# Layer 1's query-key matrices built during layer 0's fill, with the waits at the kernel's start rearranged

## The reference, cut to what matters

```python
# layer 1, attention (H = 16 heads, D = 128)
y = jnp.einsum('bnd,hde->bhne', x, Wkqv) + bkqv[None, :, None, :]
k, q, v = y[..., :D], y[..., D:2 * D], y[..., 2 * D:]
A = jnp.einsum('bhnd,bhmd->bhnm', q, k) / jnp.sqrt(jnp.float32(D))
A = softmax(where(causal, A, -inf))
out = einsum('bhnm,bhmd->bnhd', A, v).reshape(B, N, D) @ Wp + bp
```

## Time and profile before

| | us |
|---|---|
| median of three runs | 2234.11 |
| lowest, highest | 2232.35, 2235.26 |
| profiled execution | 2234.54 |
| its span, first to last instruction | 2232.8 |

### The profile page before, as it was taken

How to read it: one execution, slowest core, us unless ns; L and a number is a source line. 1 busy time by engine, 2 the same in 40 slices (tenths; PEclk the granted TensorE clock), 3 DMA queues, 4 the chain that set the end, 5 groups by cost and what they waited for, 6 DMA issues and landing times. The chain is left out here.

```text
span 2232.8 us, 60806 instructions
## 1 busy us (share of the span) xinstructions
PE 2053.9 (92%) x16256; PEld 1529.6 (69%) x16256; DVE 1781.3 (80%) x5918; ACT 1557.9 (70%) x3951; POOL 1117.5 (50%) x2439
## 2 busy tenths in 40 slices
PE   5999999996899999999999999999999993999990
PEld 3666666664677766766776776676777672999990
DVE  6899999993488888888888888888888884777775
ACT  2565656564588777878877887887777872777774
POOL 5777777775123444444344344444434434444444
PEclk7999999999899999999999999999999996999995
DMA  1000000000100000000000000000200001222226
GB/s 35 25 21 28 21 28 21 28 23 21 43 2 2 11 11 4 9 11 9 4 12 11 2 11 11 6 7 11 86 3 12 11 2 37 61 66 65 64 61 226
DMA packets 63638, 62.91 MB, mean 28 GB/s; under 512 B 9834, under 2 KB 58613, under 8 KB 62855
## 3 DMA queue, kind: packets, MB, share of 16 engines
q1 hardware_dynamic: 54906, 42.64, 6.3%
q0 software_dynamic: 8448, 16.93, 2.3%
HBM read 33.17 MB, written 22.69 MB: 25 GB/s over the span
## 5 line engine op out<-in xcount | busy, mean ns | idle before, releaser
L1373 DVE SCALAR_TENSOR_TENSOR restT<-ps_t,leadT 128x512 f16<-128x512 f32 (+1 forms) x768 | 458.7, 597 | 136.0 <-ACT leadT L1300 106.1
L1300 ACT ACTIVATE leadT<-ps_t 128x512 f16<-128x512 f32 (+1 forms) x768 | 402.2, 524 | 138.0 <-PE ps_t L1166 137.0
L1149 PE MATMUL ps_s<-xT_all,qm 128*128 128x512 f32 (+1 forms) x1024 | 489.8, 560 | 0.8 <-ACT qm L1281 0.8
L1166 PEld LDWEIGHTS ps_t<-ident,p 128*128 128x128 f32 x2560 | 316.0, 141 | 233.2 <-issue 169.4
L1166 PE MATMUL ps_t<-ident,p 128*128 128x128 f32 x2560 | 413.4, 276 | 8.0 <-DVE restT L1373 6.3
L1291 ACT ACTIVATE p<-ps_s,neg_max 128x512 f32<-128x512 f32 (+1 forms) x512 | 325.6, 636 | 80.3 <-DVE neg_max L1363 67.4
L1363 DVE CUSTOM_DVE_ANT_0 ps_s<-ps_s,mask 128x512 f32<-128x512 f32 (+1 forms) x512 | 319.9, 625 | 44.4 <-PE ps_s L1149 43.1
L993 POOL CAST v_parts<-v_all 128x36 bf16<-128x36 f32 x256 | 56.9, 222 | 562.8 <-PE ps_o L1180 562.8
L1149 PEld LDWEIGHTS ps_low<-xT_all,qm 128*128 128x128 f32 x1024 | 194.8, 190 | 135.7 <-issue 122.4
L1140 PE MATMUL ps_qm<-xT_all,m_head 128*128 128x512 f32 x512 | 264.2, 598 | 0.3 <-issue 0.3
L262 POOL TENSOR_TENSOR pv_prod<-probs,kv 128x2048 f32<-128x2048 f32 x64 | 259.3, 4072 | 3.8 <-POOL probs L254 2.3
(11 more groups left out here) (222 smaller groups left out, 4198.2 us busy)
## 6 DMA issues: line engine op xcount, KB each, us to landing
row_in<-rows_dram SPq DMA_DIRECT2D x136, 65.0 KB
y<-results SPq DMA_DIRECT2D x16, 512.0 KB, 5.2
xT<-in_xT SPq DMA_DIRECT2D x32, 128.0 KB, 2.1
xres<-in_xT SPq DMA_DIRECT2D x32, 128.0 KB, 2.1
xT_all<-x2T SPq DMA_DIRECT2D x32, 128.0 KB, 2.0
out_x<-x SPq DMA_DIRECT2D x16, 256.0 KB, 3.4
xT_all<-in_wide SPq DMA_DIRECT2D x1, 2760.0 KB
results<-row_out,row_in POOLq DMA_INDIRECT x136
```

The source lines that it names most:

```text
L1149: mm = pe.matmul(ps_s[n], qm[j][:, n * P:(n + 1) * P], xT_all[:, bass.ds(b * S, (n + 1) * P)], start=True, stop=True)
L1166: mm = pe.transpose(ps_t[g][:, at + n * P:at + (n + 1) * P], probs[i][:, n * P:(n + 1) * P], ident[:, :])
L1300: act.activation(leadT[j][g][:, :], ps_t[g][:, 0:width[g]], ACT.Copy, scale=RAISE)\
L1373: dve.scalar_tensor_tensor(out=restT[j][g][:, :], in0=ps_t[g][:, 0:width[g]], scalar=RAISE, in1=leadT[j][g][:, :], op0=ALU.mult, op1=ALU.s ...
```

## The change

1. `wq`, `wk`, `bq` are loaded by SP in layer 0, after step 0's DMAs, on a semaphore `qk_weights_in`. PE builds the matrices and the bias column at the head of its step 1 (`build_matrices`), in the banks `ps_y`, `ps_tail` and `ps_front`, which the fill does not use yet; ACT copies them at the head of its step 1 (`copy_matrices`). `project` of pair 0 waits for the four copies, `four_experts` of pair 0 for the bias. `m_all` and `mb_all` live through the stages.
2. POOL makes the constants first and sets `v_all` after them; `copy_v` of pair 0 waits for it. `consts_made` counts five.
3. `wqkv` has a semaphore of its own. PE's first four products wait for it and `xT` alone; the constants and the seven other weights are waited for after them. ACT no longer waits for the constants.
4. In `attention1` PE reads each head's matrix from `m_all`; `m_head` and `load_head` are gone. POOL splits the first head's values before it makes the route's constants, and DVE squares the centroids after the masks of head 0.

```diff
@@ layer0, SP @@
+                    if first(u, j, 0):
+                        for dst, src in ((wq, wqT), (wk, wkT), (bq_sb, bq)):
+                            sp.dma_start(dst[:, :], src).then_inc(qk_weights_in, 16)
-                sp.dma_start(wqkv_sb[:, :], wqkv).then_inc(weights_in, 16)
+                sp.dma_start(wqkv_sb[:, :], wqkv).then_inc(wqkv_in, 16)
@@ layer0, POOL @@
-                pool.memset(v_all[:, :], 1.0).then_inc(consts_made, 1)
+                pool.memset(ident[:, :], 0.0).then_inc(ident_zeroed, 1)
...
-                pool.memset(ident[:, :], 0.0).then_inc(ident_zeroed, 1)
                 pool.wait_ge(ident_zeroed, 1)
...
-                pool.wait_ge(consts_made, 6)
+                pool.memset(v_all[:, :], 1.0).then_inc(v_set, 1)
+                pool.wait_ge(consts_made, 5)
@@ layer0, PE @@
-                pe.wait_ge(consts_made, 6)
-                pe.wait_ge(weights_in, 16 * NWEIGHTS)
+                pe.wait_ge(wqkv_in, 16)
+
+                def build_matrices():
+                    pe.wait_ge(qk_weights_in, 16 * 3)
+                    for g in range(H // 4):
+                        for h in range(4 * g, 4 * g + 4):
+                            mm = pe.matmul(tile(ps_m[g], h % 4), tile(wq, h), tile(wk, h), start=True, stop=True)
+                        mm.then_inc(m_ps, 1)
+                    pe.wait_ge(m_sb, 1)
+                    for h in range(H):
+                        mm = pe.matmul(ps_m[0][:, h:h + 1], tile(wk, h), bq_sb[:, h:h + 1], start=True, stop=True)
+                    mm.then_inc(mb_ps, 1)
...
+                    if first(u, j, 0):
+                        pe.wait_ge(m_sb, H // 4)
...
+                    if first(u, j, 1):
+                        build_matrices()
...
                 qkv_products(0, 0, 0)
                 qkv_products(0, 0, 1)
+                pe.wait_ge(consts_made, 5)
+                pe.wait_ge(weights_in, 16 * NWEIGHTS)
                 steps(pe, step)
@@ layer0, ACT @@
-                act.wait_ge(consts_made, 6)
...
+                def copy_matrices():
+                    for g in range(H // 4):
+                        act.wait_ge(m_ps, g + 1)
+                        act.copy(m_all[:, g * 4 * P:(g + 1) * 4 * P], ps_m[g][:, :]).then_inc(m_sb, 1)
+                    act.wait_ge(mb_ps, 1)
+                    act.mul(mb_all[:, :], ps_m[0][:, 0:H], SCALE).then_inc(mb_sb, 1)
+
                 def step(u, j, part):
+                    if first(u, j, 1):
+                        copy_matrices()
@@ attention1 @@
-                pool.wait_ge(m_sb, H // 4)
-
-                def load_head(b, h):
-                    k = H * b + h
-                    j = h % 2
-                    when(pool, qm_ps, k - 1)
-                    pool.sem_inc(passed, 1)
-                    pool.tensor_copy(m_head[j][:, :], m_all[:, h * P:(h + 1) * P])\
-                        .then_inc(m_head_ready, 1)
...
                 def queries(b, h):
                     k = H * b + h
                     j = h % 2
-                    pe.wait_ge(m_head_ready, k + 1)
                     when(pe, qm_sb, k)
-                    pe.matmul(ps_qm[:, :], m_head[j][:, :], xT_all[:, bass.ds(b * S, S)],
+                    pe.matmul(ps_qm[:, :], blk(m_all, h), xT_all[:, bass.ds(b * S, S)],
                               start=True, stop=True).then_inc(qm_ps, 1)
```

More of the change, by code:

```diff
@@ L63, in __init__, with layer0 @@
         assert self.chunk * self.chunks == hidden and self.blocks == 4
-def layer0(nc, sh, xT_in, wqkv, wproj, bproj, gate_w, gate_b, expert_w, expert_b, wv1, keep):
-    xT_all, v_all, ident, ones = keep
+def layer0(nc, sh, xT_in, wqkv, wproj, bproj, gate_w, gate_b, expert_w, expert_b, wv1, wqT, wkT, bq, keep):
+    xT_all, v_all, ident, ones, m_all, mb_all = keep
+    SCALE = float(P) ** -0.5
     NP = sh.tiles // 2
@@ L144, in layer0 @@
         ident_zeroed = sem("ident_zeroed")
-        weights_in = sem("weights_in")
+        weights_in, wqkv_in, v_set = sem("weights_in"), sem("wqkv_in"), sem("v_set")
+        qk_weights_in, m_ps, m_sb, mb_ps, mb_sb = (
+            sem("qk_weights_in"), sem("m_ps"), sem("m_sb"), sem("mb_ps"), sem("mb_sb"))
         xT_loaded = [sem(f"xT_loaded{j}") for j in range(2)]
@@ L188, in before, with first @@
             return u + (j - k) // 2, (j - k) % 2
+        def first(u, j, s):
+            return isinstance(u, int) and 2 * u + j == s
         v_heads = v_all[:, :].rearrange("p (b h k c) -> p b h k c", h=H, k=sh.blocks, c=DH + 1)
@@ L368, in four_experts @@
                     s = 2 * u + j
+                    if first(u, j, 0):
+                        pe.wait_ge(mb_sb, 1)
                     when(pe, gated_ready, 4 * s + 2 * a + half - 1)
@@ L546, in copy_v @@
                     act.wait_ge(v_ps, s + 1)
+                    if first(u, j, 0):
+                        act.wait_ge(v_set, 1)
                     for a in range(2):
@@ L588, in _ @@
             def _(dve):
-                dve.wait_ge(consts_made, 6)
+                dve.wait_ge(consts_made, 5)
                 def by_head(t, n=H):
@@ L753, with attention1 @@
 NOWHERE = 1 << 22
-def attention1(nc, sh, wqT, wkT, bq, wp, wpT, bp, bv1, cT, keep, routing, expert_loads):
-    xT_all, v_all, ident = keep
+def attention1(nc, sh, wp, wpT, bp, bv1, cT, keep, routing, expert_loads):
+    xT_all, v_all, ident, m_all, mb_all = keep
     rows_dram, tile_expert, tile_row = routing
@@ L781, in sem @@
             return ctx.enter_context(nc.semaphore(name))
-        wq = sb("wq_sb", [P, H * P])
-        wk = sb("wk_sb", [P, H * P])
-        bq_sb = sb("bq_sb", [P, H])
-        m_all = sb("m_all", [P, H * P])
-        mb_all = sb("mb_all", [P, H])
-        m_head = [sb(f"m_head{j}", [P, P]) for j in range(2)]
         mask = sb("mask", [P, S])
@@ L1120, in _ @@
             def _(pe):
-                pe.wait_ge(weights_in, 48)
-                for g in range(H // 4):
-                    for h in range(4 * g, 4 * g + 4):
-                        mm = pe.matmul(ps_m[g][:, (h % 4) * P:(h % 4 + 1) * P], wq[:, h * P:(h + 1) * P],
-                                       wk[:, h * P:(h + 1) * P], start=True, stop=True)
-                    mm.then_inc(m_ps, 1)
-                for h in range(H):
-                    mm = pe.matmul(ps_qm[:, h:h + 1], wk[:, h * P:(h + 1) * P], bq_sb[:, h:h + 1],
-                                   start=True, stop=True)
-                mm.then_inc(mb_ps, 1)
-                pe.wait_ge(m_sb, H // 4)
-                pe.wait_ge(mb_sb, 1)
                 def queries(b, h):
@@ L1267, in _ @@
             def _(act):
-                for g in range(H // 4):
-                    act.wait_ge(m_ps, g + 1)
-                    act.copy(m_all[:, g * 4 * P:(g + 1) * 4 * P], ps_m[g][:, :]).then_inc(m_sb, 1)
-                act.wait_ge(mb_ps, 1)
-                act.mul(mb_all[:, :], ps_qm[:, 0:H], SCALE).then_inc(mb_sb, 1)
-                act.wait_ge(mb_sb, 1)
                 def copy_queries(b, h):
@@ L1950, in two_layers @@
             v_all = three_stages.enter_context(nc.sbuf_tensor("v_all", [P, sh.tiles * H * (DH + 1)], F32))
-            layer0(nc, sh, xT, wqkv, wproj, bproj, gate_w, gate_b, expert_w, expert_b, wv1,
-                   (xT_all, v_all, ident, ones))
+            m_all = three_stages.enter_context(nc.sbuf_tensor("m_all", [P, H * P], F32))
+            mb_all = three_stages.enter_context(nc.sbuf_tensor("mb_all", [P, H], F32))
+            layer0(nc, sh, xT, wqkv, wproj, bproj, gate_w, gate_b, expert_w, expert_b, wv1, wqT, wkT, bq,
+                   (xT_all, v_all, ident, ones, m_all, mb_all))
             wide_sb = xT_all[:, 0:E * sh.wide]
@@ L1957, in two_layers @@
             expert_loads = ((wide_sb, wide), (w2_sb, w2))
-            attention1(nc, sh, wqT, wkT, bq, wp, wpT, bp, bv1, cT, (xT_all, v_all, ident), routing,
+            attention1(nc, sh, wp, wpT, bp, bv1, cT, (xT_all, v_all, ident, m_all, mb_all), routing,
                        expert_loads)
```

70 lines of the change are left out of this document (32 added, 38 removed).

## The result

The changed kernel takes 2211.49 us, the median of four runs (2207.62 to 2212.74); the kernel before, in four runs beside it, 2233.47 (2232.35 to 2235.26). The ratio is 0.9895, interval 0.9882 to 0.9908, so the change takes 22 us away. Forecast were 2210.5 us and a range of 2205 to 2218. The profiled execution took 2211.51 us with a span of 2209.8, 23.0 less than that of before.

What follows compares the result with a forecast made beforehand. It took PE to fill the loops, leaving the layer boundary and first 40 us, where no engine is full. Boundary -19.0, loop 0, start -6.2, build +1.5 gave -23.7: 2210.8, or 2210.4 against the median; stated 2210.5, range 2205 to 2218.

Steps and rivals of the forecast that it cites:

- The boundary: Between layer 0 and layer 1: first query product directly after the barrier, at 555.65 instead of 574.64, gaining 19.0 us.
- +-1.3: Layer 1's first products: PE's clock rising sooner wins 1.3 us, later loses 1.0; zero was taken.
- The start: Kernel's start: PE waits only for `wqkv` and `xT`, starting at about 3.6 instead of 9.83, gaining 6.2 us.
- DVE's term: Kernel's start: DVE's first product follows PE at the same distance, at 7.1 instead of 13.34.
- The step by which ACT's table load follows PE at the same distance as in before: Kernel's start: ACT's table load and copy keep their distance behind PE's first product, so DVE starts at 7.1.
- The bound of 2.9 us for DVE beside the clear of `v_all`: Kernel's start: DVE's first product overlaps POOL's clear from 7.1 to 10; the whole overlap bounds the loss.
- The build in the fill: Layer 0's fill: matrices built on PE from 13.5 to 24.2, making the head sums late by 1.5 us.
- the prediction's bounds, 0 and 6.8: Lateness in layer 0's fill: 0 with full clock from 24; 6.8 us with half clock through the build too.
- The loop: Layer 1's loop: removing 256 POOL copies gains 0; bounds 3 us won, 1 us lost.
- rival (b): Layer 1's loop: without POOL's copies 4 to 8 us of PE's stalls go, total 2204; chance 0.08.
- Rival (a): Layer 0's fill: the build eats the start's gain, lateness 6 us instead of 1.5, total 2215; chance 0.20.
- Rival (d): Layer 1's query products: reading from `m_all` exposes PE's weight load, costing 49 us, total 2259; chance 0.02.

Runs made afterwards that it cites:

- A: Chip of the result and of the profile before: kernel before 2233.47 us, changed kernel 2211.49 us.
- C: Chip of the second group of follow-up runs: kernel before 2234.20 us, changed kernel run again 2210.69 us, ratio 0.9891.
- D: Chip of the third group of follow-up runs: kernel before 2234.53 us; changed kernel with `m_head` put back 2209.30 us (one run).
- B: Chip of the first group of follow-up runs: kernel before 2257.18 us; changed kernel with `m_head` put back 2234.68 us, ratio 0.9900.

## Why the prediction was right

**The boundary: right to the tenth.** Forecast -19.0 with 1.3 either way for the clock; 18.97 measured. The first product follows the barrier at once, 2.2 us behind the end of ACT's last copy, and nothing that was moved (the constants, the centroids' squares, the five DMAs) made DVE late: its first mask came 5.1 us behind the first product, in before 5.2. The clock: after, half speed lasted until 559.2, 7.6 us behind the first product, where it was 8.2 in before; the loop is as long as before. So neither end of the +-1.3 was used.

**The start: PE right, DVE's term mis-sized by 1.3 us.** PE at 3.69 for 3.6. The step by which ACT's table load follows PE at the same distance as in before failed. In before the table load came behind PE's first product; in after it is at 0.79. The run with ACT's wait put back shows the cause: with that wait, DVE starts at 7.31. The Trainium skill, "ScalarE: Activation LUTs" (What ACT_TABLE_LOAD costs), measures 1283 ns for the load, and this trace's 1.28 us agrees; its step-by-step section says that the compiler puts the load right before the activation, and the traces add which wait stands in front of it. The start without the build was worth 7.3 us at the first statistics instead of 6.2.

The bound of 2.9 us for DVE beside the clear of `v_all` was not needed: DVE's two products took 4.49 us beside POOL's 7.77 us clear, as they did alone in before. By the Trainium skill, "SBUF — State Buffer" (Who interferes with whom), a DVE instruction with at most one SBUF input, outside its two-port modes, doesn't contend with GpSimd; the trace agrees, for a clear that only writes. The same page's rule on two SBUF inputs was weighed in the prediction by the division into `sa`, which ran 172 to 192 ns with the copies and 173 to 192 without. That row can't test the rule: in before none of the 256 divisions overlaps a copy of `m_head` (the copy at 1000.07 ends at 1000.36, the division next to it starts at 1001.29). What shows no price of the copies on A, by this rule or another, is the loop, 1266.4 us with the copies and 1266.5 without.
```profile
L1389 DVE TENSOR_TENSOR sa<-out_sum,recip x256: 173/181/192, 568.8 to 1829.7; 128x32 f32<-128x32 f32 x128
```

**The build in the fill: the mechanism right, the size wrong.** The prediction named the queue (build, qkv products, sums, qkv products, sums) and worked out two sizes: 3.4 us late with the clock at half throughout, and 1.5 if it rose in the first sums. It took 1.5. The build's own length held (14.79 to 25.5, 10.7 us, as put). Measured are 3.6 on A (34.28 against 30.67) and 4.7 on C. The term that was mis-sized is the clock's: the prediction expected a single rise, by the one in before at 33.3. What came was a rise in the build and a fall in the bias products. Also, `bq` landed at 14.79, 1.3 later than put. With the same order on PE the lateness was 0.3 and 0.6 us on D, where the clock stayed full, and 1.3 and 1.7 on B. So 1.5 lies within what this stream does, but no single value could have been right for it; the prediction's bounds, 0 and 6.8, hold all of them.

**The loop: right on A, for a reason that was only half seen.** Nobody waits for the copies, so 0: that held, with +0.1 us. But a wait list with no entry tells that the cover suffices, not how thick it is. It was 0.2 us a head here. On B POOL goes on 0.5 us later after each scatter, and there the kernels without the copies have a loop 13 to 14.5 us shorter than those with them: rival (b), more than it allowed for, on another chip. There the kernel with only ACT's wait restored was 37.5 us faster than before, where before and after differ by 22 on A.

**The sum.** -19.0 and 0 held; start and build, -6.2 + 1.5 = -4.7, came as -7.3 + 3.6 = -3.7, and -4.0 at the barrier. Two errors of over 1 us in opposite directions left 0.7 in the sum, 2211.5 for 2210.8 in the profiled execution. That the total was within 1 us is therefore better than its terms deserve. Rival (a), the build eating the start's gain, happened in part: 3.6 us of lateness where it had 6. Rival (d), an exposed weight load, did not: PE's loads for the query product take 192 ns in the median and 190 to 191 with the copies, and the loop is as long.

## What to carry to other kernels

A step that is in no wait list still has a margin: read how long before its use it ends (here 0.2 us), since a chip on which a neighbour on its queue is slower turns it into a wait (76 times in 256 heads on B), and the removal that is worth nothing on one chip is worth 13 to 14.5 us on another. Work moved into an engine's idle time is free only as far as the next product on that queue can still start when its data come: put the pieces that nobody needs soon (here the bias column) behind those that the next engine waits for. Before a lateness is put down to the length of a piece, look for the same order in other profiles: here it cost 0.3 to 4.7 us, by the clock that the pieces got. And when a wait is taken off a stream, look at what stood between it and the first real instruction, such as a table load.

## What the runs showed of the hardware

- After an indirect DMA whose record is 0.96 us on every chip, POOL's next instruction came 0.3 us later on D and A and 0.80 on B (medians of 56), with nothing in the trace on B to name it but an output product that had ended 0.84 us before. Before itself took 2257 us there against 2234. That this delay is all of B's difference isn't shown: the kernels without copies have a loop of 1271.4 us on B, 5 more than on A.
- By the products' durations the clock rose in the build, near 19.9 on A and 21.3 on C, and it fell at 23.3 and 24.8, in the bias products both times (20.90 to 25.5, 21.95 to 26.2); on D the same instructions of the fill, in the kernel with `m_head` back, ran at full clock from the build's last matrices to 33.0, and the statistics were at 30.96. So the first statistics moved by up to 4.4 us for the same instructions. Why the clock fell in some profiles and not in others is not settled.
- At the kernel's start, ahead of the first clock record, the clock column reads 1.00, while the products take the times of half speed (16 head sums 3.67 us in the kernel with the start alone, against 1.91 after its clock record at 26.8). The durations of a known product are the safer reading there.
